# Reordering the tail of an attention-pooling kernel: a last load in two halves, and a different order of TensorE's closing steps

## The chip, the cores and the metric

The kernel runs on one core of one Trainium2 chip. The metric is the device time of one execution in microseconds (us), from the first to the last thing the core does; less is better.

## The reference

512 rows, each with 200 behaviours of 128 numbers and one candidate of 128 numbers. For each row an attention over the 200 behaviours is computed, the behaviours are summed with its weights, and the sum goes with the candidate through a small two-layer network to one logit.

```python
B, S, E = (512, 200, 128)             # ATT_H = 128, MLP_H = 256, all float32
W_b, W_c = (fc1_w[:E], fc1_w[E:])
h = relu(einsum('bse,eh->bsh', behavior_emb, W_b) + (candidate_emb @ W_c)[:, None, :] + fc1_b)
scores = einsum('bsh,h->bs', h, fc2_w[:, 0]) + fc2_b[0]
attn = softmax(scores, axis=-1)
user_interest = einsum('bse,bs->be', behavior_emb, attn)
x = concatenate([user_interest, candidate_emb], axis=1)
z = relu(x @ mlp1_w + mlp1_b)
logit = (z @ mlp2_w + mlp2_b)[:, 0]
```

## The kernel before

**Tiling.** The 512 rows are taken in 32 chunks of 16 rows (`CHUNKS` is 32, `LAST` is 31). Each chunk is loaded twice, 1.6 MB each time: once transposed (`xt`, for the first product and the scores) and once in its own layout (`x`, 128 partitions of 25 tiles of 128 numbers, for the weighted sum). SyncE issues both kinds from one queue, four buffers of each kind. The own layout of a chunk is loaded by `load`, which waits until the sum of the chunk four earlier has released its buffer.

**The loop.** In the period of chunk c TensorE does the first product of chunk c (`products`), the scores of chunk c-1 and the weighted sum of chunk c-3. ScalarE and VectorE make the high and low halves of the transposed data, the relu and the softmax. GpSimd spreads the exponentials over a block mask (`mask_weights`), so that a matmul with them as weights sums each row apart. Every second chunk the sums are copied from PSUM to SBUF by ScalarE (`copy_pooled4`), folded and transposed by a product with a mask (`transpose_sums`), and copied again (`copy_pooled_t`).

**The tail.** After the loop every engine has its own order written out by hand; it runs it strictly as written, and semaphores alone tie the engines together. The rows are in two parts (`PART_CHUNKS`): part 0 is chunks 0 to 27 (448 rows), part 1 is chunks 28 to 31 (64 rows). For each part TensorE does:

- `row_sums` (L702): sums of the exponentials; VectorE then takes reciprocals and spreads them (`inverses`, L502 and L505), and `spread_inverses` (L708) brings them to all partitions.
- `mlp_candidates` (L721): the candidate's half of the first layer, for m = 0 and 1 (two halves of the 256 hidden units).
- `normalise` on VectorE (L515): the transposed sums times the inverses.
- `mlp_pooled` (L727): the pooled half of the first layer, onto the same banks, then a relu: on ScalarE for part 0 (`relu`, L378), on VectorE for part 1 (`last_relu`, L572).
- `logits` (L734), then an add on VectorE (L589) and a store issued by SyncE (L279), for part 0 first.

`weighted_sum_alone` does the sums of chunks 30 and 31, which fill one bank between them; each is one call of `sum_tiles` over 25 tiles, or two calls for the last chunk (13 tiles, then the rest). Its weights come from `mask_last` on VectorE (L564), in the same two runs. Then the last chain starts: `copy_pooled4(LAST)`, `transpose_sums(LAST)`, `copy_pooled_t(LAST)`, `normalise(1)`, `mlp_pooled(1, m)`, `last_relu`, `logits(1)`, the add, the store. One float32 matmul stands in the trace as two records of MATMUL (PE) and two of LDWEIGHTS (PEld).

Of the kernel before, what the change touches and what calls it, by code (L numbers as in the profile page):

```python
# [7 lines left out]
ALU = mybir.AluOpType  # L8
# [3 lines left out]
P = 128  # L12
# [3 lines left out]
ROWS = P // PARTS  # L16
# [6 lines left out]
TILES = 25  # L23
# [12 lines left out]
LAG = 3  # L36
# [24 lines left out]
def attention_pooling_kernel(nc, behavior, behavior_t, cand_rest, weights_1, first, masks, later, out):  # L61
# [13 lines left out]
    with ExitStack() as ctx:  # L75
# [3 lines left out]
        def sem(name):  # L79
            return ctx.enter_context(nc.semaphore(name))  # L80
# [71 lines left out]
        xt_loaded = [sem(f"xt_loaded{i}") for i in range(XT_BUFS)]  # L152
        x_loaded = [sem(f"x_loaded{i}") for i in range(X_BUFS)]
        xt_half = sem("xt_half")
        weights_1_loaded = sem("weights_1_loaded")
        first_loaded = sem("first_loaded")
        masks_loaded = sem("masks_loaded")
# [73 lines left out]
        @block.sync  # L231
        def _(sp):
            arrivals = [*xt_piece, xt_loaded[0]]
            for g, arrived in enumerate(arrivals):
                sp.dma_start(xt[0][:, g, :], behavior_t[0, :, g, :]).then_inc(arrived, 16)
            sp.dma_start(cand_t[:, P:], cand_rest).then_inc(cand_rest_loaded, 16)
            for half, arrived in enumerate([xt_half, xt_loaded[1]]):
                mine = slice(2 * half, 2 * half + 2)
                sp.dma_start(xt[1][:, mine, :], behavior_t[1, :, mine, :]).then_inc(arrived, 16)
                if half == 0:  # L240
                    sp.dma_start(masks_sb[:, :], masks).then_inc(masks_loaded, 16)

            def load_transposed(c, buf):


                if buf is None:
                    buf = c
                elif isinstance(c, int) and c < XT_BUFS + WHOLE:
                    sp.wait_ge(z_done, (c - XT_BUFS + 1) * GROUPS)
                else:  # L250
                    sp.wait_ge(xl_made, (c - XT_BUFS + 1 - WHOLE) * GROUPS)
                sp.dma_start(xt[buf][:, :, :], behavior_t[c, :, :, :]).then_inc(xt_loaded[buf], 16)

            def load(c, buf):

                if buf is None:
                    buf = c
                else:
                    sp.wait_ge(pooled_done, c + (1 - X_BUFS))
                sp.dma_start(x[buf][:, :], behavior_v[c, :, :]).then_inc(x_loaded[buf], 16)  # L260


            for c in range(2, X_BUFS):
                load_transposed(c, None)
            load(0, None)
            sp.dma_start(later_sb[:, :], later).then_inc(later_loaded, 16)
            for c in range(X_BUFS, 2 * X_BUFS):
                load_transposed(c, c - X_BUFS)
                load(c - LAG, None if c - LAG < X_BUFS else c - LAG - X_BUFS)
            with sp.Fori(0, CHUNKS // X_BUFS - 2) as turn:  # L270
                for j in range(X_BUFS):
                    c = turn * X_BUFS + (2 * X_BUFS + j)
                    load_transposed(c, j)
                    load(c - LAG, (j - LAG) % X_BUFS)
            for c in range(CHUNKS - LAG, CHUNKS):
                load(c, c % X_BUFS)
            for part, (a, b) in enumerate(PART_CHUNKS):
                sp.wait_ge(logit_made, part + 1)
                sp.dma_start(out[a * ROWS:b * ROWS].rearrange("(g n) -> g n", g=GROUPS),  # L279
                             logit[0:P:Q, part, 0:quarter[part]]).then_inc(stored, 16)  # L280
            sp.wait_ge(stored, 2 * 16)
# [31 lines left out]
        def _(act):  # L313
# [26 lines left out]
            def copy_pooled4(c, bank):  # L340
                act.wait_ge(pooled_done, c + 1)
                nc.scalar.copy(pooled4[:, :], bank[:, 0:P]).then_inc(pooled4_copied, 2)
# [72 lines left out]
            copy_pooled4(LAST - 2, u_ps)  # L415
            copy_pooled_t(LAST - 2, u_ps[:, P:P + 2 * ROWS])
            exponents(LAST, LAST % 2, False)
            copy_pooled4(LAST, last_pair_ps)
            copy_pooled_t(LAST, last_pair_ps[:, P:P + 2 * ROWS])
            relu(0)  # L420
            relu(1)

        @block.vector
        def _(dve):
# [130 lines left out]
                next_low(2)  # L555

            periods(period)(dve)
            def mask_last(run):
                a, b = [0, LAST_RUN, TILES][run:run + 2]
                buf = LAST % 2  # L560
                if run == 0:
                    dve.wait_ge(weights_made, LAST + 1)
                    dve.wait_ge(pooled_done, LAST - 1)
                nc.vector.tensor_tensor(  # L564
                    weights_by_row[buf][:, a:b, pair_half[buf]],
                    weights[buf][:, a:b].unsqueeze(2).to_broadcast([P, b - a, ROWS]),
                    row_mask.unsqueeze(1).to_broadcast([P, b - a, ROWS]), ALU.mult).then_inc(last_masked, 1)

            def last_relu(m):
                a, b = PART_CHUNKS[1]  # L570
# [5 lines left out]
            inverses(0, 2)  # L576
            for n in range(SOFTMAX_STEPS):
                softmax(LAST, LAST % 2, n, False)
            mask_last(0)
            mask_last(1)  # L580
            inverses(1, 1)
            normalise(0)
            inverses(1, 2)
            normalise(1)
            last_relu(0)
            last_relu(1)
            for part in range(2):
                dve.wait_ge(logit_done, part + 1)
                nc.vector.tensor_scalar(logit[:, part, 0:quarter[part]], logit_ps[part][:, 0:quarter[part]], b_out, None,  # L589
                                        ALU.add).then_inc(logit_made, 1)  # L590

        @block.tensor
        def _(pe):
# [73 lines left out]

            def weighted_sum_alone(c):
                q = c % X_BUFS
                pe.wait_ge(x_loaded[q], loads(c, q))  # L670
                if q % 2 == 0:

                    pe.wait_ge(relu_made, LAST * HALF + 1)
                    pe.wait_ge(masked, c + 1)
                    sum_tiles(c, q, last_pair_ps, 0, WHOLE_TILES, GROUPS - 1).then_inc(pooled_done, 1)
                else:
                    pe.wait_ge(last_masked, 1)
                    sum_tiles(c, q, last_pair_ps, 0, LAST_RUN, None)
                    pe.wait_ge(last_masked, 2)
                    sum_tiles(c, q, last_pair_ps, LAST_RUN, WHOLE_TILES, LAST_RUN).then_inc(pooled_done, 1)  # L680

            def transpose_sums(c, summed):
# [94 lines left out]
            score(LAST, LAST % 2, False)  # L777
            transpose_sums(LAST - 2, u_ps[:, P:P + 2 * ROWS])
            spread_inverses(0)
            weighted_sum_alone(LAST - 1)  # L780
            mlp_candidates(1, 0)
            row_sums(1)
            weighted_sum_alone(LAST)
            spread_inverses(1)
            mlp_candidates(0, 0)
            mlp_candidates(0, 1)
            mlp_candidates(1, 1)
            transpose_sums(LAST, last_pair_ps[:, P:P + 2 * ROWS])
            mlp_pooled(0, 0)
            mlp_pooled(0, 1)  # L790
            mlp_pooled(1, 0)
            mlp_pooled(1, 1)
            logits(0)
            logits(1)


# [50 lines left out]
```

## Time and profile before

| what | value |
|---|---|
| time, median of 3 runs | 266.75 us (266.53 to 266.75) |
| time of the profiled execution | 266.47 us |
| its span, first to last instruction | 264.7 us |
| PE busy | 259.3 us, 98% of the span |
| DVE busy | 224.2 us, 85% |
| ACT busy | 200.6 us, 76% |
| queue of the large loads, share of 16 DMA engines' span | 94.7% |
| share of the last chain on PE | 60% |
| granted TensorE clock, mean | 1.000 |

The span is what the profiler records from the first to the last instruction; the time has 1.8 us more around it. PE is TensorE's matmuls, PEld its weight loads, DVE VectorE, ACT ScalarE, SPq SyncE's queue. The ends of matmuls are modelled, so that a busy PE shows starts better than ends.

### The profile page before, as it was taken

The page shows a single profiled execution, that of the slowest core. Times are in us where ns is not written, and L with a number is a line of the kernel's source. Part 1 is how long each engine was busy: PE and PEld are TensorE (multiplying, and loading weights), DVE is VectorE, ACT ScalarE, POOL GpSimd, SP SyncE. Part 2 cuts the span into 40 slices and gives each one's busy share as a digit, 9 for nine tenths or more (in the row PEclk, how much of TensorE's full clock was granted, in tenths as well). Part 3 has the DMA queues.
Part 4 walks back from the last instruction along what each step waited for, and adds up shares of the span by engine and source line. Part 5 has one row for each costly group of instructions (what it writes and reads, how often), then busy time and mean ns, then how long its engine had stood idle before and what let it go on. Part 6 is the DMA issues. An engine that isn't in the chain of part 4 may idle for free.

```text
span 264.7 us, 10384 instructions
## 1 busy us (share of the span) xinstructions
PE 259.3 (98%) x3942; PEld 212.4 (80%) x3942; DVE 224.2 (85%) x397; ACT 200.6 (76%) x481; POOL 29.4 (11%) x38
## 2 busy tenths in 40 slices
PE   8999999999999999999999999999999999999995
PEld 7557788888888868888888888888888888888973
DVE  0479998999898988989899998989989898999541
ACT  2569888798887697878789887878888787889312
POOL 2003001111110111110111111011111100111100
PEclk9999999999999999999999999999999999999999
DMA  7999999999999999999999999999999999999900
GB/s 247 430 433 422 422 426 420 424 424 420 426 422 423 426 420 429 429 426 426 424 429 429 426 426 426 428 428 422 428 429 428 426 426 426 429 428 426 391 32 0
DMA packets 10544, 105.87 MB, mean 400 GB/s; under 512 B 1184, under 2 KB 1696, under 8 KB 2592
## 3 DMA queue, kind: packets, MB, share of 16 engines
q1 hardware_dynamic: 10240, 105.44, 94.7%
q8 instruction: 12, 0.20, 0.3%
q10 hardware_dynamic: 288, 0.20, 0.2%
q14 instruction: 4, 0.03, 0.0%
HBM read 105.63 MB, written 0.00 MB: 399 GB/s over the span
## 4 chain that ended last, share of the span: by engine, by line
PE 60%; DMA 18%; DVE 14%; issue 4%; ACT 1%; DVEq 1%; POOL 0%; ACTq 0%; SPq 0%; POOLq 0%
DMA xt<-in_behavior_t 18%; PE s_ps L632 12%; PE u_ps L643 11%; PE z_ps L617 10%; PE z_ps L613 9%; DVE xl L454 9%; PE z_ps L614 8%; DVE hidden L464 5%; PE z_ps L608 4%; PE z_ps L750 2%; PE z_ps L643 1%; ACT xh L329 1%; PE z_ps L684 1%; PE z_ps L727 1%; PE z_ps L721 1%
## 5 line engine op out<-in xcount | busy, mean ns | idle before, releaser
L454 DVE TENSOR_TENSOR xl<-xt,xh 128x800 fp32r<-128x800 f32 x120 | 123.2, 1047 | 8.9 <-ACT xh L329 8.7
L329 ACT CAST xh<-xt 128x800 fp32r<-128x800 f32 x120 | 100.4, 862 | 34.2 <-DMA xt<-in_behavior_t 33.1
L371 ACT ACTIVATE hidden<-z_ps,bias 128x200 f32<-128x200 f32 x256 | 88.3, 428 | 7.4 <-PE z_ps L608 3.6
L613 PE MATMUL z_ps<-xh,w_hi 128*128 128x512 f32 x240 | 86.4, 360 | 0.5 <-DVE hidden L464 0.5
L614 PE MATMUL z_ps<-xh,w_lo 128*128 128x512 f32 x240 | 79.4, 345 | 0.0
L464 DVE TENSOR_TENSOR hidden<-z_ps,neg_bias 128x800 f32<-128x800 f32 x64 | 62.9, 982 | 3.3 <-PE z_ps L608 2.0
L617 PE MATMUL z_ps<-xl,w_hi 128*128 128x512 f32 x240 | 64.8, 351 | 0.9 <-DVE xl L454 0.2
L613 PEld LDWEIGHTS z_ps<-xh,w_hi 128*128 128x128 f32 x240 | 45.0, 188 | 16.3 <-issue 6.0
L299 POOL TENSOR_TENSOR weights_by_row<-weights,masks_sb 128x400 f32<-128x400 f32 x31 | 27.6, 890 | 218.3 <-ACT weights L336 177.3
L632 PE MATMUL s_ps<-hidden,f_col 128*3 128x160 f32 (+4 forms) x1280 | 50.1, 301 | 0.0
L614 PEld LDWEIGHTS z_ps<-xh,w_lo 128*128 128x128 f32 x240 | 45.1, 188 | 5.6
L643 PE MATMUL u_ps<-x,weights_by_row 128*32 128x128 f32 (+1 forms) x1680 | 46.7, 262 | 0.0
L643 PEld LDWEIGHTS u_ps<-x,weights_by_row 128*32 128x32 f32 x1680 | 42.3, 110 | 1.1
L632 PEld LDWEIGHTS s_ps<-hidden,f_col 128*3 128x3 f32 (+4 forms) x1280 | 32.3, 90 | 11.6 <-issue 4.2
L617 PEld LDWEIGHTS z_ps<-xl,w_hi 128*128 128x128 f32 x240 | 38.0, 188 | 4.1 <-DVE xl L454 4.0
L475 DVE STREAM_TRANSPOSE scores<-s_ps 128x160 f32<-128x160 f32 x32 | 10.9, 339 | 3.3 <-PE s_ps L632 3.1
L336 ACT ACTIVATE weights<-scores,exp_bias 128x25 f32<-128x25 f32 x32 | 10.9, 340 | 3.3 <-DVE exp_bias L493 3.3
L608 PE MATMUL z_ps<-xt,weights_sb 128*128 128x512 f32 (+1 forms) x32 | 11.9, 516 | 0.0
L608 PEld LDWEIGHTS z_ps<-xt,weights_sb 128*128 128x128 f32 x32 | 6.1, 199 | 5.1 <-issue 4.4
L493 DVE SCALAR_TENSOR_TENSOR exp_bias<-row_max,shift 128x1 f32<-128x1 f32 x32 | 7.0, 220 | 3.4
L483 DVE STREAM_TRANSPOSE part_max_t<-part_max 128x32 f32<-128x32 f32 x32 | 6.8, 213 | 1.1
L489 DVE STREAM_TRANSPOSE row_max<-row_max_t 128x32 f32<-128x32 f32 x32 | 6.8, 212 | 1.1
(65 smaller groups left out, 77.6 us busy)
## 6 DMA issues: line engine op xcount, KB each, us to landing
x<-in_behavior SPq DMA_DIRECT2D x32, 1600.0 KB, 26.6
xt<-in_behavior_t SPq DMA_DIRECT2D x30, 1600.0 KB, 23.7
xt<-in_behavior_t SPq DMA_DIRECT2D x4, 400.0 KB, 4.9
xt<-in_behavior_t SPq DMA_DIRECT2D x2, 800.0 KB, 7.7
later_sb<-in_later SPq DMA_DIRECT2D x1, 258.5 KB, 19.6
first_sb<-in_cand_rest SPq DMA_DIRECT2D x1, 192.0 KB, 5.7
first_sb<-in_first ACTq DMA_DIRECT2D x1, 128.0 KB, 4.8
masks_sb<-in_masks SPq DMA_DIRECT2D x1, 114.0 KB, 6.8
```

The costliest lines, as they stand in the source:

```text
L299: nc.gpsimd.tensor_tensor(weights_by_row[buf][:, :, pair_half[buf]], weights[buf][:, :].unsqueeze(2).to_broadcast([P, TILES, ROWS]), row_m ...
L329: nc.scalar.copy(xh[g][:, :], xt[q][:, g, :]).then_inc(xh_made, 1)
L336: nc.scalar.activation(weights[buf][:, :].rearrange("p (r t) -> p r t", t=RUN), score_runs(buf), ACT.Exp, bias=exp_bias[buf][:, :], accum_ ...
L371: op = nc.scalar.activation(hidden[q % 2][:, g, :, mine], z[:, :, mine], ACT.Relu, bias=bias[:, bass.ds(c * ROWS + g * EACH + b, 1)])
L454: nc.vector.tensor_tensor(xl[g][:, :], xt[q][:, g, :], xh[g][:, :].bitcast(F32), ALU.subtract).then_inc(xl_made, 1)
L464: nc.vector.tensor_tensor(hidden[q % 2][:, g, :, :].rearrange("p t (b s) -> p t b s", s=PARTS), z, nb.to_broadcast([P, TILES, EACH, PARTS] ...
L608: op = nc.tensor.matmul(z[:, a:b], w_b, xt[q][:, g, a:b], start=True, stop=True)
L613: nc.tensor.matmul(z[:, a:b], w_hi[:, :], xh[g][:, a:b], start=True, stop=False)
L614: nc.tensor.matmul(z[:, a:b], w_lo[:, :], xh[g][:, a:b], start=False, stop=False)
L617: op = nc.tensor.matmul(z[:, a:b], w_hi[:, :], xl[g][:, a:b], start=False, stop=True)
L632: op = nc.tensor.matmul(s_ps[g * Q:g * Q + rows, 0:RUN * Q].rearrange("p (t s) -> p t s", s=Q), f2_col[:, 0:rows], hidden[buf][:, g, r * R ...
L643: return nc.tensor.matmul(bank[g * Q:(g + 1) * Q, cols], weights_by_row[buf][:, t, :], x[q][:, t * E + cols.start:t * E + cols.stop], star ...
```

## The change

The own layout of chunk 31 is loaded by two transfers instead of one: tiles 0 to 12 with a semaphore of their own (`x_half`), then tiles 13 to 24. `mask_last` makes the weights in one instruction instead of two. The orders of the tail change on three engines:

- TensorE: all four `mlp_candidates` stand ahead of the sum of chunk 30; `mlp_pooled(0, ·)`, `row_sums(1)` and `spread_inverses(1)` stand between the sums of chunks 30 and 31; `logits(0)` stands directly behind the sum of chunk 31, ahead of `transpose_sums(LAST)`.
- ScalarE: the two `relu` of part 0 stand ahead of the two last copies.
- VectorE: `normalise(0)` stands ahead of the mask, `inverses(1, ·)` follow it, and the add of part 0's logits stands ahead of `normalise(1)`.

```diff
@@ sync
-            for c in range(CHUNKS - LAG, CHUNKS):
+            for c in range(CHUNKS - LAG, LAST):
                 load(c, c % X_BUFS)
+            sp.wait_ge(pooled_done, CHUNKS - X_BUFS)
+            cols = LAST_RUN * E
+            sp.dma_start(x[LAST % X_BUFS][:, 0:cols], behavior_v[LAST, :, 0:cols]).then_inc(x_half, 16)
+            sp.dma_start(x[LAST % X_BUFS][:, cols:], behavior_v[LAST, :, cols:]).then_inc(x_loaded[LAST % X_BUFS], 16)
@@ scalar
             exponents(LAST, LAST % 2, False)
+            relu(0)
+            relu(1)
             copy_pooled4(LAST, last_pair_ps)
             copy_pooled_t(LAST, last_pair_ps[:, P:P + 2 * ROWS])
-            relu(0)
-            relu(1)
@@ vector
-            mask_last(0)
-            mask_last(1)
+            normalise(0)
+            mask_last()
             inverses(1, 1)
-            normalise(0)
             inverses(1, 2)
+            add_out_bias(0)
             normalise(1)
             last_relu(0)
             last_relu(1)
-            for part in range(2):
-                dve.wait_ge(logit_done, part + 1)
-                nc.vector.tensor_scalar(logit[:, part, 0:quarter[part]], logit_ps[part][:, 0:quarter[part]], b_out, None,
-                                        ALU.add).then_inc(logit_made, 1)
+            add_out_bias(1)
@@ tensor, weighted_sum_alone
-                pe.wait_ge(x_loaded[q], loads(c, q))
                 if q % 2 == 0:
+                    pe.wait_ge(x_loaded[q], loads(c, q))
...
                 else:
+                    pe.wait_ge(x_half, 16)
                     pe.wait_ge(last_masked, 1)
                     sum_tiles(c, q, last_pair_ps, 0, LAST_RUN, None)
-                    pe.wait_ge(last_masked, 2)
+                    pe.wait_ge(x_loaded[q], loads(c, q))
                     sum_tiles(c, q, last_pair_ps, LAST_RUN, WHOLE_TILES, LAST_RUN).then_inc(pooled_done, 1)
@@ tensor, the order
             spread_inverses(0)
+            for part in range(2):
+                for m in range(2):
+                    mlp_candidates(part, m)
             weighted_sum_alone(LAST - 1)
-            mlp_candidates(1, 0)
-            row_sums(1)
-            weighted_sum_alone(LAST)
-            spread_inverses(1)
-            mlp_candidates(0, 0)
-            mlp_candidates(0, 1)
-            mlp_candidates(1, 1)
-            transpose_sums(LAST, last_pair_ps[:, P:P + 2 * ROWS])
             mlp_pooled(0, 0)
             mlp_pooled(0, 1)
+            row_sums(1)
+            spread_inverses(1)
+            weighted_sum_alone(LAST)
+            logits(0)
+            transpose_sums(LAST, last_pair_ps[:, P:P + 2 * ROWS])
             mlp_pooled(1, 0)
             mlp_pooled(1, 1)
-            logits(0)
             logits(1)
```

## Rows read from the trace of the kernel before

**Rows 1.** Chain that ended last, in order of time: start us, us, what.
```profile
255.13 1.53 PE z_ps L643 x52
```

**Rows 2.** The issue of chunk 31's own layout, by line: duration ns, start us, time to landing.
```profile
L260 SPq DMA_DIRECT2D x<-in_behavior x1: 328/328/328, 238.7 to 238.7; - x1
DMA to landing us min/median/max: 15.3/15.3/15.3
```

**Rows 3.** Timeline of the tail, TensorE: start us, us, engine, line, op, tiles, count.
```profile
253.01 1.58 PE L643 MATMUL z_ps<-x,weights_by_row 128*32 128x128 f32 x56
254.52 0.43 PE L721 MATMUL s_ps<-first_sb,later_sb 128*128 128x64 f32 x2
254.79 0.34 PE L702 MATMUL z_ps<-weight_sums,masks_sb 128*128 128x4 f32 x2
255.06 1.60 PE L643 MATMUL z_ps<-x,weights_by_row 128*32 128x128 f32 x56
256.59 0.43 PE L708 MATMUL z_ps<-inv_sel,ones 128*128 128x64 f32 x2
256.86 1.72 PE L721 MATMUL z_ps<-first_sb,later_sb 128*128 128x448 f32 x4
258.42 0.33 PE L721 MATMUL u_ps<-first_sb,later_sb 128*128 128x64 f32 x2
258.59 0.36 PE L684 MATMUL z_ps<-masks_sb,pooled 128*128 128x32 f32 x2
258.78 1.75 PE L727 MATMUL z_ps<-pooled_n,later_sb 128*128 128x448 f32 x4
260.37 0.33 PE L727 MATMUL s_ps<-pooled_n,later_sb 128*128 128x64 f32 x2
260.86 0.87 PE L734 MATMUL z_ps<-z_all,later_sb 128*1 128x112 f32 x32
261.26 0.35 PEld L734 LDWEIGHTS z_ps<-z_all,later_sb 128*1 128x1 f32 x24 [0.30 <-ACT z_all L378]
```

**Rows 4.** Timeline of the tail, VectorE and ScalarE, columns as in the group above.
```profile
247.76 0.99 DVE L464 TENSOR_TENSOR hidden<-z_ps,neg_bias 128x800 f32<-128x800 f32 x1 [0.89 <-PE z_ps L617]
...
252.33 0.18 ACT L346 COPY pooled_t<-u_ps 128x32 f32<-128x32 f32 x1 [1.48 <-PE u_ps L684]
...
254.01 0.64 DVE L564 TENSOR_TENSOR weights_by_row<-weights,masks_sb 128x208 f32<-128x208 f32 x2 [0.50 <-ACT weights L336]
...
255.16 0.18 DVE L502 RECIPROCAL inv_sums<-z_ps 128x4 f32<-128x4 f32 x1 [0.51 <-PE z_ps L702]
255.26 0.60 DVE L515 TENSOR_TENSOR pooled_n<-z_ps,pooled_t 128x448 f32<-128x448 f32 x1
255.78 0.22 DVE L505 TENSOR_TENSOR inv_sel<-inv_sums,masks_sb 128x64 f32<-128x64 f32 x1
...
256.76 0.27 ACT L342 COPY pooled<-z_ps 128x128 f32<-128x128 f32 x1 [2.78 <-PE z_ps L643]
...
259.04 0.18 ACT L346 COPY pooled_t<-z_ps 128x32 f32<-128x32 f32 x1 [2.01 <-PE z_ps L684]
...
259.33 0.22 DVE L515 TENSOR_TENSOR pooled_n<-z_ps,pooled_t 128x64 f32<-128x64 f32 x1 [3.33 <-ACT pooled_t L346]
...
259.82 1.39 ACT L378 ACTIVATE z_all<-z_ps,later_sb 128x448 f32<-128x448 f32 x2 [0.59 <-PE z_ps L727]
...
260.74 0.28 DVE L572 TENSOR_SCALAR z_all<-s_ps,later_sb 128x64 f32<-128x64 f32 x1 [1.19 <-PE s_ps L727]
...
260.96 0.28 DVE L572 TENSOR_SCALAR z_all<-u_ps,later_sb 128x64 f32<-128x64 f32 x1
...
261.70 0.48 DVE L589 TENSOR_SCALAR logit<-z_ps,later_sb 128x112 f32<-128x112 f32 x2 [0.45 <-PE z_ps L734]
```

**Rows 5.** The two final adds and the two stores, by line: ns min/median/max, first and last start.
```profile
L589 DVE TENSOR_SCALAR logit<-z_ps,later_sb x2: 226/280/334, 261.7 to 261.9; 128x112 f32<-128x112 f32 x1, 128x16 f32<-128x16 f32 x1
L279 SPq DMA_DIRECT2D out_logit<-logit x2: 507/580/654, 262.1 to 262.8; - x2
```

More of the change, by code:

```diff
@@ L154, in attention_pooling_kernel @@
         xt_half = sem("xt_half")
+        x_half = sem("x_half")
         weights_1_loaded = sem("weights_1_loaded")
@@ L557, in _, with mask_last @@
             periods(period)(dve)
-            def mask_last(run):
-                a, b = [0, LAST_RUN, TILES][run:run + 2]
+            def mask_last():
                 buf = LAST % 2
-                if run == 0:
-                    dve.wait_ge(weights_made, LAST + 1)
-                    dve.wait_ge(pooled_done, LAST - 1)
+                dve.wait_ge(weights_made, LAST + 1)
+                dve.wait_ge(pooled_done, LAST - 1)
                 nc.vector.tensor_tensor(
-                    weights_by_row[buf][:, a:b, pair_half[buf]],
-                    weights[buf][:, a:b].unsqueeze(2).to_broadcast([P, b - a, ROWS]),
-                    row_mask.unsqueeze(1).to_broadcast([P, b - a, ROWS]), ALU.mult).then_inc(last_masked, 1)
+                    weights_by_row[buf][:, :, pair_half[buf]],
+                    weights[buf][:, :].unsqueeze(2).to_broadcast([P, TILES, ROWS]),
+                    row_mask.unsqueeze(1).to_broadcast([P, TILES, ROWS]), ALU.mult).then_inc(last_masked, 1)
             def last_relu(m):
@@ L578, in _, with add_out_bias @@
                 softmax(LAST, LAST % 2, n, False)
-            mask_last(0)
-            mask_last(1)
+            normalise(0)
+            mask_last()
             inverses(1, 1)
-            normalise(0)
             inverses(1, 2)
+            def add_out_bias(part):
+                dve.wait_ge(logit_done, part + 1)
+                nc.vector.tensor_scalar(logit[:, part, 0:quarter[part]], logit_ps[part][:, 0:quarter[part]], b_out, None,
+                                        ALU.add).then_inc(logit_made, 1)
+            add_out_bias(0)
             normalise(1)
```

## The prediction

> **What bounds the kernel now.** I read the page first, for the shares of the span: PE is busy nearly throughout, and the queue of the large loads is almost as full, so which of the two holds the end has to be read from the end itself. The chain that ended last says it: the sum of chunk 31 is on it as work of PE that begins where the PE work before it stops, at 255.13, and not behind a transfer [rows 1]. The load of chunk 31 was issued at 238.7 and landed 15.3 us later, at 254.0 [rows 2], while its first matmul began at 255.06, 0.27 behind the start of the instruction before it, the row sums of part 1 [rows 3]. That distance is what any such instruction takes to get past. So chunk 31's data were 1.1 us early. The weights for it, the mask on VectorE, were whole at 254.65 [rows 4], 0.4 early. What sets the tail is TensorE's own order: from 253.01 to 261.3 there is only one hole on it, the 0.30 ahead of the second half of the logits, where it waited for ScalarE's relu [rows 3]. The serial chain of the last chunk (copy, transpose, copy, normalise) runs meanwhile on the other engines under PE's candidate and pooled products of part 0, and so costs nearly nothing. I therefore rebuild the tail in the new order, instruction by instruction, from 253.01 on. Nothing before that moves: the load's issue at 238.7 is the first edit in time, and it has no other load behind it.
>
> **The transfers.** One issue becomes two, some 0.33 us more on SyncE's queue [rows 2], with only the stores behind them. The same bytes, so the second half lands at about 254.0. Bounds: nothing gained below, and above, if the smaller rows were slow, one landing more late by the whole 15.3. The first half was wanted at 255.06 and will be wanted at 259.2 (below), so I price it at nothing; the cover is now 5 us deep. Doing without cover, each us of lateness beyond it would cost a us.
>
> **The mask.** 208 and 192 elements took 0.64 in two instructions [rows 4]; one of 400 is less than the 0.60 that 448 elements take [rows 4]. `normalise(0)` (0.60) goes ahead of it, so the mask is ready about 0.6 us later, near 255.2. Wanted at 259.2: nothing. `normalise(0)` itself is ready near 254.2, or at the latest by 255.9 as before, and wanted at 256.46: nothing.
>
> **TensorE up to the sum of chunk 31.** The candidates may start at once: the last relu of VectorE on the bank ended at 248.75, and the copy that frees the last bank at 252.51 [rows 4]. From 253.01:
> - candidates: the four passes of 448 columns took 258.42 - 256.86 = 1.56, the two small products 0.21 and 0.17 [rows 3]. To 254.95.
> - sum of chunk 30: 254.52 - 253.01 = 1.51 [rows 3]. To 256.46.
> - `mlp_pooled(0, ·)`: 260.37 - 258.78 = 1.59 [rows 3]. To 258.05. The relus (0.63 each, two in 1.39 with their gap [rows 4]) begin 1.04 after its start as before (258.78 to 259.82), run from 257.5 to 258.9 and are done long before the logits.
> - `row_sums(1)` at 258.05. Here the new order makes a stall: `spread_inverses(1)` now follows it directly and needs VectorE's reciprocal and spreading of its result. Before, the whole sum of chunk 31 (1.53) stood between the two and covered this. Row sums to reciprocal 255.16 - 254.79 = 0.37; reciprocal 0.18; spreading 0.22 [rows 3, 4]; two hand-overs of 0.03 to 0.05, as from ScalarE's relu, done at 261.21, to PE at 261.26 [rows 3, 4]. Sum 0.85, so `spread_inverses(1)` starts at 258.90. Of this 0.27 is what the row sums took anyway; the stall is 0.58. Behind it waits the sum of chunk 31, which needs nothing of it. Bounds: 0.4 if the modelled ends of PE flatter the 0.37, 0.8 if each hand-over costs 0.1 more. I take 0.58, all of whose parts but the hand-overs have rows of the same instructions.
> - its 0.27 (256.59 to 256.86 [rows 3]) and the sum of chunk 31 starts at 259.17, 4.11 later than before.
>
> A rule of the Trainium skill bears on the stall: "TensorE: Matmul & The Clock Gate", The mechanism, says that TensorE can pull weight loads ahead of matmuls in flight when they go to another part of the array. Held against a semaphore wait it would have the first weights of the sum ready under the stall and give back an estimated 0.1 to 0.2. The row speaks against it: at 261.26 the weight loads of the logits too began only with the wait's end, after 0.30 of nothing [rows 3]. The sum goes by the row.
>
> **From there to the end.** Durations and distances are those of the same instructions before.
> - last matmul of the sum ends 1.60 after its start: 260.77. ScalarE's copy starts 0.10 later (256.66 to 256.76) and takes 0.27: 261.14. `logits(0)` fills this hole: its half of the first group took 0.30, the whole second batch of 24 loads 0.35 [rows 3], so it is issued by about 261.1 and costs nothing; without it PE would only idle. Its relus and inputs are ready.
> - transpose at 261.19; copy starts 0.45 after it (258.59 to 259.04) and takes 0.18: 261.82 [rows 3, 4].
> - `normalise(1)` 0.11 later, takes 0.22: 262.15 [rows 4]. The add of part 0's logits (0.33 [rows 5]), new in front of it on VectorE, runs from 261.2 to 261.5, before its input is there: nothing. Its store (0.65 [rows 5]) is out of the way by 262.3.
> - `mlp_pooled(1, 0)` at 262.20; relu 0.37 later (260.37 to 260.74), the second 0.22 after that and 0.28 long: 263.07 [rows 3, 4].
> - `logits(1)`, second half, at 263.12, result after 0.30: add at 263.42, 0.23 long [rows 5]: 263.65.
> - one store: issued at 263.68, 0.51 as the second one took, or 0.65 as the first [rows 5]: 264.19. From the end of the last issue (262.8 + 0.5 = 263.3) to the span's end at 264.7 it was 1.4: 265.6.
>
> **The sum.** Before, the end of chunk 31's sum (256.66) to the end of the span was 8.0; after, it is 265.6 - 260.77 = 4.8. So 3.2 are taken out behind the sum and 4.1 put in front of it. Of the 4.1, 3.5 is PE work that before filled the waits of the last chain; that chain is now bare. Net +0.9 us: 0.58 by the stall, the rest by waits that lie open after the transpose (262.20 against 261.4, when PE is free, and 262.6 to 263.1 for the relus), less what one store less at the very end saves (before, the second store was issued 0.7 behind the first). On the profiled execution that is 266.47 + 0.9 = 267.4; the median of the runs stands 0.28 above that execution, so the forecast is 266.75 + 0.9 = **267.7 us**, slower by 0.35%.
>
> **The rivals.** A measurement of this kernel tells some 0.2%, 0.53 us, from no change.
> - *A, the forecast: the bare chain and the stall, +0.9.* Its own range is 267.3 to 268.1: the stall at 0.4 or 0.8, the store's issue at 0.65 (+0.14), and a few hundredths on each of seven hand-overs either way. Chance 0.72.
> - *B, no change that can be told.* The hand-overs between engines in the new tail sum to some 0.5 (0.10, 0.05, 0.09, 0.11 and so on); were all 0.03, 0.3 would go, and with the stall at 0.4 the loss is 0.4: 267.2. For it speaks that the ends of matmuls are modelled; against it, that the starts on VectorE and ScalarE, which I used, are not. Chance 0.17.
> - *C, faster: the load was late after all.* This is one mechanism: if chunk 31's data land L us after 254.0, the kernel before pays L - 1.1 and the kernel after nothing until L is 5. It breaks even at L = 2.0 and is faster by over 0.2% from L = 2.5; at L = 3 the new kernel stands 1.0 below the old. Against it: all timed runs lie within 0.3 of the profiled one, in which it was 1.1 early, so none can have had an L above 1.4. With the L of 2.5 to 3 that a gain needs, the time would be some 266.0 against the 266.75. Chance 0.06. Perfetto Trace Analysis of the Trainium skill, DMA Optimizations, says that splitting a transfer can let work start sooner if DMA engines are generally idle. By that rule alone this rival would be favoured; the queue that is full to 94.7% of the span does not meet its condition, and the sum did not wait.
> - *D, much slower: the halves are slow.* If the shorter rows made the second half land after 259.2 plus the 0.8 that the first 13 tiles take, over 5 us late, every further us counts: with 2 us more 269.7. The rows of 12.8 KB become rows of 6.7 and 6.1 KB, and no row shown here has a loss of that kind. Chance 0.05.
>
> **How the numbers follow.** A, B, C and D have 0.72, 0.17, 0.06 and 0.05. Slower is A less the part of it under +0.53 (0.04), with D: 0.73. Within 0.2% is B with that part, less a part of B that is a small gain (0.03): 0.18. Faster is C with it: 0.09. The range reaches from 267.0, which leaves out C and a part of B, to 268.2, above A's own range and below D.
>
> **What would show it.** In the changed kernel's trace: the sum of chunk 31 starts at about 259.2, waiting for no DMA; TensorE is idle for about 0.6 ahead of L708's second use, released by VectorE's spreading; after the sum's end the chain is copy, transpose, copy, normalise, pooled, relu, logits, add, store, with PE idle for 0.8 ahead of the last pooled products and some 0.4 ahead of the last logits; the last add ends near 263.65 and the span is 265.6. The landing of both halves is over 4 us ahead of their use. The forecast is wrong if the stall or the bare chain is much shorter than its rows, if the old kernel in truth waited for the load, or if the split slows the queue by more than 5 us.

## The result, and the profile after

The changed kernel takes 267.72 us (median of 6 runs, 267.34 to 268.22); the kernel before 266.63 us (266.20 to 266.75) beside it. The ratio is 1.0046, 95% interval 1.0033 to 1.0060: slower by 1.2 us, or by 1.1 as the medians stand. Measured once more on another occasion it gave 1.0051 (1.0038 to 1.0064). The forecast was 267.7 us, slower by 0.35%.

First the tail of the changed kernel as a timeline, TensorE's weight loads left out, with the columns of [rows 3]. Lines have moved by a few: L649 is the weighted sum (L643 before), L709 the row sums, L715 the spreading of the inverses, L728 and L734 the candidate and the pooled products, L741 the logits, L691 the transpose.

```profile
252.95 1.67 PE L728 MATMUL z_ps<-first_sb,later_sb 128*128 128x448 f32 x4
...
254.04 0.58 DVE L567 TENSOR_TENSOR weights_by_row<-weights,masks_sb 128x400 f32<-128x400 f32 x1
...
254.94 1.58 PE L649 MATMUL z_ps<-x,weights_by_row 128*32 128x128 f32 x56
...
256.45 1.77 PE L734 MATMUL z_ps<-pooled_n,later_sb 128*128 128x448 f32 x4
...
258.06 0.28 PE L709 MATMUL z_ps<-weight_sums,masks_sb 128*128 128x4 f32 x2
...
258.37 0.18 DVE L507 RECIPROCAL inv_sums<-z_ps 128x4 f32<-128x4 f32 x1 [3.75 <-PE z_ps L709]
258.59 0.23 DVE L510 TENSOR_TENSOR inv_sel<-inv_sums,masks_sb 128x64 f32<-128x64 f32 x1
...
258.87 0.43 PE L715 MATMUL z_ps<-inv_sel,ones 128*128 128x64 f32 x2 [0.54 <-DVE inv_sel L510]
...
259.24 1.60 PE L649 MATMUL z_ps<-x,weights_by_row 128*32 128x128 f32 x56
...
260.63 0.59 PE L741 MATMUL z_ps<-z_all,later_sb 128*1 128x112 f32 x16
260.94 0.27 ACT L347 COPY pooled<-z_ps 128x128 f32<-128x128 f32 x1 [2.05 <-PE z_ps L649]
...
261.35 0.38 PE L691 MATMUL z_ps<-masks_sb,pooled 128*128 128x32 f32 x2
...
261.82 0.18 ACT L351 COPY pooled_t<-z_ps 128x32 f32<-128x32 f32 x1 [0.62 <-PE z_ps L691]
262.11 0.23 DVE L520 TENSOR_TENSOR pooled_n<-z_ps,pooled_t 128x64 f32<-128x64 f32 x1 [0.51 <-ACT pooled_t L351]
...
262.39 0.43 PE L734 MATMUL s_ps<-pooled_n,later_sb 128*128 128x64 f32 x2 [0.66 <-DVE pooled_n L520]
...
262.87 0.28 DVE L575 TENSOR_SCALAR z_all<-s_ps,later_sb 128x64 f32<-128x64 f32 x1 [0.53 <-PE s_ps L734]
...
263.20 0.45 PE L741 MATMUL z_ps<-z_all,later_sb 128*1 128x16 f32 x16 [0.15 <-DVE z_all L575]
263.72 0.23 DVE L589 TENSOR_SCALAR logit<-z_ps,later_sb 128x16 f32<-128x16 f32 x1 [0.35 <-PE z_ps L741]
```

TensorE now waits three times: 0.54 for VectorE's inverses, with the ready sum of chunk 31 queued behind it; 0.66 ahead of the last pooled products; 0.15 ahead of the last logits. A fourth gap, of 0.13 ahead of the transpose, is put down to no engine by the profile. Before, its only hole was 0.30 long [rows 3]. The sum of chunk 31 starts 4.18 later than in [rows 3] (259.24 against 255.06), and from its start to the last add's it is 4.5 against 6.8 (261.9 [rows 5] less 255.06): 2.4 won behind it, 4.2 paid in front. Of the 1.8 by which the last add is late, the store's issue, which no longer stands in a queue, gives back 0.6.

The two halves of the load, by line (duration ns, start us, time to landing):

```profile
L280 SPq DMA_DIRECT2D x<-in_behavior x1: 327/327/327, 238.8 to 238.8; - x1
...
DMA to landing us min/median/max: 13.5/13.5/13.5
...
L281 SPq DMA_DIRECT2D x<-in_behavior x1: 433/433/433, 239.2 to 239.2; - x1
...
DMA to landing us min/median/max: 14.9/14.9/14.9
```

They landed at 252.3 and 254.1; the whole chunk had landed at 254.0 [rows 2]. Split or whole, the last byte comes at the same time within 0.1, and now lies 5 us ahead of its use. The two stores, by line:

```profile
L284 SPq DMA_DIRECT2D out_logit<-logit x2: 508/572/636, 261.6 to 264.0; - x2
```

The first store is out of the way by 262.3, and the second starts straight behind the last add, where before it began 0.7 behind the first [rows 5].

### The profile page after: what moved, and what is told of

It reads as the page before. It is cut to its first block, busy times and chain, and to the rows that moved or that the text cites. A ratio compares the mean times of both kernels' runs of the same rounds, so it can differ in the third digit from the quotient of the medians.

```text
span 265.9 us, 10384 instructions
## 1 busy us (share of the span) xinstructions
PE 259.5 (98%) x3942; PEld 212.2 (80%) x3942; DVE 224.6 (84%) x396; ACT 199.9 (75%) x481; POOL 29.4 (11%) x38
## 4 chain that ended last, share of the span: by engine, by line
PE 75%; DMA 11%; DVE 10%; issue 2%; DVEq 0%; ACT 0%; SPq 0%; ACTq 0%
PE s_ps L638 15%; PE u_ps L649 13%; PE z_ps L623 13%; PE z_ps L619 13%; PE z_ps L620 11%; DMA xt<-in_behavior_t 9%; DVE xl L459 5%; PE z_ps L614 4%; DVE hidden L469 3%; DMA weights_sb<-in_weights 2%; PE z_ps L649 1%; PE z_ps L691 1%; PE z_ps L734 1%; PE z_ps L728 1%; PE z_ps L715 0%
## 5 line engine op out<-in xcount | busy, mean ns | idle before, releaser
L649 PE MATMUL u_ps<-x,weights_by_row 128*32 128x128 f32 (+1 forms) x1680 | 46.7, 262 | 0.0
L649 PEld LDWEIGHTS u_ps<-x,weights_by_row 128*32 128x32 f32 x1680 | 42.3, 110 | 1.1
```

Of the source, the lines that this page charges most:

```text
L649: return nc.tensor.matmul(bank[g * Q:(g + 1) * Q, cols], weights_by_row[buf][:, t, :], x[q][:, t * E + cols.start:t * E + cols.stop], star ...
```

## The experiments

Theory 1 is the prediction's: the loss is the stall ahead of `spread_inverses(1)` and the last chain, bare of TensorE work. Theory 2: one of the other edits costs the time, above all the split load with its shorter rows. Ratios are to the kernel before on the same chip.

**The split alone.** The kernel before, with chunk 31's load in two halves:

```diff
-            for c in range(CHUNKS - LAG, CHUNKS):
+            for c in range(CHUNKS - LAG, LAST):
                 load(c, c % X_BUFS)
+            sp.wait_ge(pooled_done, CHUNKS - X_BUFS)
+            cols = LAST_RUN * E
+            sp.dma_start(x[LAST % X_BUFS][:, 0:cols], behavior_v[LAST, :, 0:cols]).then_inc(x_half, 16)
+            sp.dma_start(x[LAST % X_BUFS][:, cols:], behavior_v[LAST, :, cols:]).then_inc(x_loaded[LAST % X_BUFS], 16)
@@ weighted_sum_alone
-                pe.wait_ge(x_loaded[q], loads(c, q))
                 if q % 2 == 0:
+                    pe.wait_ge(x_loaded[q], loads(c, q))
...
                 else:
+                    pe.wait_ge(x_half, 16)
                     pe.wait_ge(last_masked, 1)
                     sum_tiles(c, q, last_pair_ps, 0, LAST_RUN, None)
                     pe.wait_ge(last_masked, 2)
+                    pe.wait_ge(x_loaded[q], loads(c, q))
```

> The kernel before with nothing changed but the load of chunk 31, which comes in two halves, with their two waits. Theory 1 (the loss is the bare chain and the stall on TensorE): the second half still lands near 254, over 1 us ahead of its use, so within 0.2 us of the kernel before. Theory 2 (the two shorter-rowed transfers cost the time): most of the 1.1 us is here, 267.4 to 267.9 us.

Measured 266.77 us, ratio 1.0013 (1.0004 to 1.0022). That is 0.3 us more, a small but distinguishable part, not the 1.1 of theory 2. Its trace does not show a place for it. The second half's landing, by line, and the sum's start in the timeline:

```profile
L281 SPq DMA_DIRECT2D x<-in_behavior x1: 434/434/434, 239.2 to 239.2; - x1
...
DMA to landing us min/median/max: 14.9/14.9/14.9
```

```profile
255.13 1.60 PE L648 MATMUL z_ps<-x,weights_by_row 128*32 128x128 f32 x56
```

Landing at 254.1, start at 255.13, no wait: the span was the 264.7 of before. Since the next run but one has the same split and stands at 1.0003, and their intervals overlap, I do not take the 0.3 as shown to be the split's.

**The stall.** The changed kernel, with the row sums one step earlier:

```diff
+            row_sums(1)
             mlp_pooled(0, 0)
             mlp_pooled(0, 1)
-            row_sums(1)
             spread_inverses(1)
```

> The changed kernel with row_sums(1) moved ahead of mlp_pooled(0, m), so that VectorE's reciprocal and spreading run under 1.6 us of TensorE's work. Theory 1: the idle time of 0.54 us ahead of spread_inverses(1) is gone and everything behind it comes 0.5 to 0.6 us earlier, 0.5 us faster than the changed kernel. Rival (TensorE's idle time there is not on the path, because a transfer or the weights hold the sum of chunk 31): under 0.2 us.

Measured 267.11 us, ratio 1.0024 (1.0015 to 1.0033), against 1.0046 and 1.0051 for the changed kernel: 0.6 to 0.7 us given back, about the size of the hole, and 0.1 more than expected. The timeline of TensorE there, spreading and then sum:

```profile
258.46 0.33 PE L715 MATMUL z_ps<-inv_sel,ones 128*128 128x64 f32 x2
...
258.72 1.60 PE L649 MATMUL z_ps<-x,weights_by_row 128*32 128x128 f32 x56
```

No wait stands behind L715, and the sum starts at 258.72 instead of 259.24. The rival, for which the sum had been held by something else, falls. Here the two weight loads of the spreading began apart, at 258.08 and 258.46; in the changed kernel both began only with the wait's end:

```profile
258.87 0.30 PEld L715 LDWEIGHTS z_ps<-inv_sel,ones 128*128 128x128 f32 x2 [0.62 <-DVE inv_sel L510]
```

**The bare chain.** The changed kernel, with all its other edits, but TensorE's work put back behind the sum of chunk 31. ScalarE's relus and VectorE's add of part 0's logits also go back to their old places, which this cut does not show:

```diff
             weighted_sum_alone(LAST - 1)
-            mlp_pooled(0, 0)
-            mlp_pooled(0, 1)
             row_sums(1)
-            spread_inverses(1)
             weighted_sum_alone(LAST)
-            logits(0)
+            spread_inverses(1)
+            mlp_pooled(0, 0)
             transpose_sums(LAST, last_pair_ps[:, P:P + 2 * ROWS])
+            mlp_pooled(0, 1)
             mlp_pooled(1, 0)
             mlp_pooled(1, 1)
+            logits(0)
             logits(1)
```

> The changed kernel with the split load, the one mask, the early normalise(0) and the early candidates kept, but mlp_pooled(0, m), spread_inverses(1) and logits(0) put back behind the sum of chunk 31, where they lie under the last chain, and the orders of ScalarE and of the two last adds put back with them. Theory 1: both the stall and the bare chain are gone, within 0.2 us of the kernel before, 1.1 us faster than the changed one. Theory 2 (transfer, mask or candidates cost the time): it stays at the changed kernel's 267.7.

Measured 266.60 us, ratio 1.0003 (0.9994 to 1.0012): the whole loss is gone, with the split load, the single mask, the early `normalise(0)` and the early candidates still in. This is the run that decides between the theories. With the run before it, it also divides the loss: 0.6 to 0.7 us for the stall (1.0046 or 1.0051 to 1.0024), and 0.6 for the bare chain (1.0024 to 1.0003). In its timeline the last chain again runs under work:

```profile
258.57 0.27 ACT L347 COPY pooled<-z_ps 128x128 f32<-128x128 f32 x1 [4.46 <-PE z_ps L649]
...
258.67 0.97 PE L734 MATMUL z_ps<-pooled_n,later_sb 128*128 128x448 f32 x2
...
259.48 0.30 PE L691 MATMUL z_ps<-masks_sb,pooled 128*128 128x32 f32 x2
...
259.62 1.00 PE L734 MATMUL z_ps<-pooled_n,later_sb 128*128 128x448 f32 x2
259.87 0.19 ACT L351 COPY pooled_t<-z_ps 128x32 f32<-128x32 f32 x1 [1.04 <-PE z_ps L691]
...
260.45 0.42 PE L734 MATMUL s_ps<-pooled_n,later_sb 128*128 128x64 f32 x2
```

The copy lies under the spreading and the first pooled product, the second copy and `normalise(1)` under the second. From the sum's start (256.87 in that trace) to the last add's it is 5.1, longer than the 4.5 of the changed kernel, and yet the whole is faster, as the sum starts 2.4 earlier: a shorter chain behind the sum is not the aim, a TensorE without holes is.

**Where logits(0) stands.** The run on the stall, with `logits(0)` behind the transpose:

```diff
             weighted_sum_alone(LAST)
-            logits(0)
             transpose_sums(LAST, last_pair_ps[:, P:P + 2 * ROWS])
+            logits(0)
```

> The changed kernel with row_sums(1) early, as in the run on the stall (267.1), and logits(0) moved from ahead of transpose_sums(LAST) to behind it, where TensorE otherwise waits 0.8 us for VectorE. If logits(0) held up the transpose, which began 0.14 us behind the end of ScalarE's copy where 0.05 would do, this gives back 0.1 us: 267.0. If the transpose waits for the copy alone, no difference from 267.1.

Measured 267.52 us, ratio 1.0028 (1.0018 to 1.0038): no gain. The expected 0.1 was wrong on its premise, since the hand-over from the copy to the transpose stayed 0.14 with nothing in front of it. Against the run on the stall it is 0.1 to 0.2 slower (1.0028 and 1.0024), which the intervals do not tell apart. Something new came in the profiled execution, at 267.70 one of the slower ones, seen in the timelines of the three engines:

```profile
260.51 0.27 ACT L347 COPY pooled<-z_ps 128x128 f32<-128x128 f32 x1 [1.13 <-PE z_ps L649]
...
260.92 0.38 PE L691 MATMUL z_ps<-masks_sb,pooled 128*128 128x32 f32 x2 [0.51 <-ACT pooled L347]
...
261.39 0.18 ACT L351 COPY pooled_t<-z_ps 128x32 f32<-128x32 f32 x1 [0.62 <-PE z_ps L691]
261.86 0.33 DVE L589 TENSOR_SCALAR logit<-z_ps,later_sb 128x112 f32<-128x112 f32 x1 [4.29 <-PE z_ps L741]
262.11 0.21 DVE L520 TENSOR_TENSOR pooled_n<-z_ps,pooled_t 128x64 f32<-128x64 f32 x1
```

The copied sums were there at 261.57, but `normalise(1)` is queued behind the add of part 0's logits, which waits for TensorE: 0.4 lost in this trace. The add put behind `normalise(1)` again:

```diff
-            add_out_bias(0)
             normalise(1)
+            add_out_bias(0)
```

> As the run with logits(0) behind transpose_sums(LAST), but VectorE's add of part 0's logits stands behind normalise(1) again. There the add ran from 261.86 to 262.11 and normalise(1), whose input was there near 261.6, began only behind it. If that was what ate the gain, this is 0.3 to 0.4 us faster than that kernel: a ratio of about 1.0015 to before, and no more than 0.1 better than with row_sums(1) early alone. If the copy's hand-over to the transpose sets it, no difference.

Measured 267.01 us, ratio 1.0016 (1.0008 to 1.0025), 0.3 us below the run before it as expected, though the two intervals overlap, so that the times alone do not show it. Against the run on the stall (1.0024) it is 0.2 better, with overlap again. In its trace `normalise(1)` starts at 261.57, 0.10 behind the copy. Against the kernel before, what is left is, by the reading above, the bare chain.

**How deep the cover of the load is.** One more load of 1.6 MB, into a buffer that nobody reads, ahead of chunk 31's in the queue; once in the kernel before (the edit below) and once in the changed one, ahead of its two halves:

```diff
+        scratch = sb("scratch", [P, TILES * E])
...
@@ sync
-            for c in range(CHUNKS - LAG, CHUNKS):
+            for c in range(CHUNKS - LAG, LAST):
                 load(c, c % X_BUFS)
+            sp.dma_start(scratch[:, :], behavior_v[0, :, :]).then_inc(dummy_loaded, 16)
+            load(LAST, LAST % X_BUFS)
...
+            sp.wait_ge(dummy_loaded, 16)
             sp.wait_ge(stored, 2 * 16)
```

> The kernel before with one more load of 1.6 MB into a buffer that nobody reads, queued directly ahead of chunk 31's own layout. At some 425 GB/s it takes 3.8 us, so chunk 31 lands near 257.8 instead of 254.0. If the cover of this load was 1.1 us, as read from the trace of before, the kernel is 2.7 us slower, 269.1 to 269.4. If the load had already been the limit, 3.8 us slower, 270.3.

Measured 271.18 us (269.80 to 272.35), ratio 1.0191 (1.0172 to 1.0209). The median lies above both values expected, and the spread is 2.5 us where it is at most 1.0 elsewhere. The profiled execution, at 269.80, is the fastest and the only one near what was expected; its rows by line and in the timeline:

```profile
DMA to landing us min/median/max: 19.3/19.3/19.3
```

```profile
258.32 1.61 PE L648 MATMUL z_ps<-x,weights_by_row 128*32 128x128 f32 x56 [3.01 <-DMA x<-in_behavior]
```

The load, issued at 238.9, landed at 258.2, 4.2 late, and TensorE waited 3.0 for it: the cover was 1.1 to 1.2, as read from [rows 2, 3]. The span was 3.3 longer. The other four runs took 1.3 to 2.6 us more still, with mean granted TensorE clocks of 0.987 to 0.994 where the profiled one has 0.998. As an estimate from these means and the spans, they miss 3.0, 1.6, 3.0 and 1.1 us of full clock more than the profiled one does, and they took 2.3, 1.4, 2.6 and 1.3 us longer. So a clock that fell while TensorE still had work, to 1.2 instead of 2.4 GHz, is the likely cause of the excess; when it fell was not seen. The one trace has it fall only behind the last matmul, as its stretches show (us; busy time of each engine; PEclk, DMA share, GB/s):

```profile
262.00:265.00 3.00, 2.96 (x43) 1.76 (x41) 0.77 (x4) 1.45 (x3) 0.00 (x0) 1.00 0.00 0
265.00:268.00 3.00, 0.00 (x0) 0.00 (x0) 0.44 (x2) 0.00 (x0) 0.00 (x0) 0.81 0.00 1
```

> The changed kernel with the same additional load of 1.6 MB ahead of chunk 31's two halves, which then land near 257.8, while the sum of chunk 31 starts at 259.2. Theory 1 (the cover is now 5 us deep and its price is the bare chain): no slower than the changed kernel, 267.7. Rival D (the halves are on the path): up to 3.8 us slower, 271.

Measured 267.58 us, ratio 1.0039 (1.0026 to 1.0052): not slower than the changed kernel at all. The second half, issued at 239.0, needed 18.8 and landed at 257.8, still 1.3 ahead of the sum's start:

```profile
259.07 1.61 PE L653 MATMUL z_ps<-x,weights_by_row 128*32 128x128 f32 x56
```

So the change does buy something: 4 us more of cover for the last load. On this kernel nothing needs it, and it costs 1.1 us. Where the load is 4 us late the changed kernel wins by 3.6 by the medians (271.18 and 267.58), and by 2.2 against the one execution of the old kernel whose clock did not fall.

**The end of the end.** The kernel before, its second store issued from ScalarE's queue:

```diff
+        def store(eng, part):
+            a, b = PART_CHUNKS[part]
+            eng.wait_ge(logit_made, part + 1)
+            eng.dma_start(out[a * ROWS:b * ROWS].rearrange("(g n) -> g n", g=GROUPS),
+                          logit[0:P:Q, part, 0:quarter[part]]).then_inc(stored, 16)
@@ sync
-            for part, (a, b) in enumerate(PART_CHUNKS):
-                sp.wait_ge(logit_made, part + 1)
-                sp.dma_start(out[a * ROWS:b * ROWS].rearrange("(g n) -> g n", g=GROUPS),
-                             logit[0:P:Q, part, 0:quarter[part]]).then_inc(stored, 16)
+            store(sp, 0)
             sp.wait_ge(stored, 2 * 16)
@@ scalar, last
+            store(act, 1)
```

> The kernel before with the store of the last 64 rows issued from ScalarE's queue instead of SyncE's. From the rows of before, the second issue began at 262.8 because the first one, 0.65 us long, stood in front of it, while its data were there at 262.2. If the end is set by the issue and what follows it, the span is 0.5 us shorter, 266.1. Rival (the two stores share what they wait for, or ScalarE issues more slowly): within 0.2 us.

Measured 266.42 us, ratio 1.0000 (0.9991 to 1.0009). No gain; the two issues in the timeline:

```profile
262.21 0.64 SPq L234 DMA_DIRECT2D out_logit<-logit  x1
262.36 1.29 ACTq L234 DMA_DIRECT2D out_logit<-logit  x1
```

The issue from ScalarE took 1.29 and ended at 263.65, 0.35 later than two issues in a row on SyncE (263.3 [rows 5]), and yet the span was no longer (264.6 against 264.7): from the end of the last issue to the end of the span it was 0.95 here and 1.4 in the kernel before. So the recorded end of an issue is not by itself what sets the end. Then one store instead of two, with the logits of all rows in one bank, so that one add serves both:

```diff
@@ tensor, logits
-                    for g in range(GROUPS):
-                        op = nc.tensor.matmul(logit_ps[part][g * Q:g * Q + 1, 0:quarter[part]], w_out[:, m:m + 1],
-                                              z_all[:, m, bass.ds(PART_CHUNKS[part][0] * ROWS + g * quarter[part],
-                                                                  quarter[part])],
+                    first, last = (n * ROWS for n in PART_CHUNKS[part])
+                    for g in range(first // P, GROUPS):
+                        a, b = max(first, g * P), min(last, (g + 1) * P)
+                        op = nc.tensor.matmul(logit_ps[0][g * Q:g * Q + 1, a - g * P:b - g * P], w_out[:, m:m + 1],
+                                              z_all[:, m, a:b],
@@ vector (the two adds go)
...
+            dve.wait_ge(logit_done, 2)
+            nc.vector.tensor_scalar(logit[:, 0, :], logit_ps[0][:, 0:P], b_out, None, ALU.add).then_inc(logit_made, 1)
@@ sync (the two stores go)
...
+            sp.wait_ge(logit_made, 1)
+            sp.dma_start(out.rearrange("(g n) -> g n", g=GROUPS), logit[0:P:Q, 0, :]).then_inc(stored, 16)
+            sp.wait_ge(stored, 16)
```

> The kernel before with all 512 logits in one bank (part 1's 16-column pieces become one piece of 64 in the same bank), one add and one store instead of two of each. Two store issues of 0.65 and 0.51 us stood one behind the other, and issuing the second from ScalarE's queue did not help, as it took 1.3 us beside the first. Theory: the store's issue starts as before, about 262.1, and nothing is queued behind it: the span ends 0.5 us earlier, 265.9 to 266.0. Rival (a store of 128 columns is issued or lands more slowly, or the 0.5 is lost in what follows): within 0.2 us.

Measured 266.07 us, ratio 0.9979 (0.9971 to 0.9988): 0.6 us faster than before. The store was issued at 262.46 and not at 262.1 as expected, since it now waits for the one add, and the issue ended at 263.11. From the start of the logits to the end of the span the trace has 3.4 us (264.5 - 261.12) against 3.8 before (264.7 - 260.86 [rows 3]), which places 0.5 of the 0.6. The same on top of the order of the run on the bare chain:

> The changed kernel with mlp_pooled(0, m) and spread_inverses(1) back behind the sum of chunk 31 (266.6, as before) and with the one add and one store of the run that gave 0.6 us. If the two are independent, the gain is the same 0.5 to 0.6 and perhaps 0.1 more, since TensorE's last hole was 0.21 there and not 0.30: 266.0. If the gain came from another order of the old kernel's end, it is not here: 266.6.

Measured 265.90 us, ratio 0.9976 (0.9967 to 0.9986), the fastest of all, though not distinguishable from the run above. The end of its timeline:

```profile
261.92 0.35 DVE L589 TENSOR_SCALAR logit<-z_ps,later_sb 128x128 f32<-128x128 f32 x1 [0.47 <-PE z_ps L736]
262.30 0.64 SPq L283 DMA_DIRECT2D out_logit<-logit  x1
```

The one issue ends at 262.94, against 263.3 for the second of two [rows 5], and the span is 264.4 against 264.7: this trace, of an execution at 266.15, places 0.3 of the gain.

The changed kernel was also run once more, beside the kernel above and the one with the add behind `normalise(1)`:

> The changed kernel once more, on the same chip as the two below: its ratio to the kernel before was 1.0046 (1.0033 to 1.0060); by theory 1 it stands some 1.0 to 1.2 us above before, and 0.5 to 0.6 above the kernel with row_sums(1) early.

Measured 267.93 us, ratio 1.0051 (1.0038 to 1.0064), 1.3 us above before, just over the 1.0 to 1.2 expected, and 0.9 above the kernel with the row sums early, `logits(0)` and the add moved, measured beside it; 0.5 to 0.6 was expected to the run on the stall, which was not in this measurement.

## Why the prediction was right

The direction, the two causes and the size came out as forecast: +0.9 us, measured +1.1 to 1.2. That the forecast of 267.7 meets the measured 267.72 is partly luck. It was reckoned on a median of 266.75 for the kernel before, and the kernel before measured beside the changed one had 266.63; the lower base and the 0.2 to 0.3 by which the loss was under-priced hide each other in part.

**The bound.** The sum of chunk 31 was read as waiting for TensorE's order and not for the load, with 1.1 us to spare. The late-load run measured that cover: 4.2 late, 3.0 waited. Rivals C (the load was late after all) and D (the halves are slow) are out: the split alone lands at 254.1, and no kernel without the extra load waited for a transfer there. (For D the prediction has "over 5 us late"; by its own numbers, 259.2 + 0.8 - 254.0, it is 6.) Rival B (hand-overs so short that the loss drowns) is out too: they were longer than taken, not shorter.

**TensorE up to the sum.** Forecast start 259.17, measured 259.24. Candidates to 254.94 (254.95 forecast), sum of chunk 30 to 256.45 (256.46), row sums at 258.06 (258.05), spreading at 258.87 (258.90). These times flatter it a little, as the tail of this trace began 0.06 earlier than in the kernel before (252.95 against 253.01). The stall was priced at 0.58, TensorE's rows have 0.54, and removing it gave 0.6 to 0.7. The weight loads of the sum were not pulled under the wait: with the wait over at 258.87, TensorE took 0.37 until the sum began, 0.10 more than the 0.27 taken from the rows, and the loads of the spreading's own weights, which nothing had to compute, began only at 258.87 too. By the rule of the Trainium skill that the prediction weighed ("TensorE: Matmul & The Clock Gate", The mechanism) 0.1 to 0.2 of that might have gone; this trace agrees with the rows of before and does not show weight loads pulled ahead past a wait for another engine.

**From the sum to the end.** Forecast 4.8 from the end of the sum to the end of the span, measured 265.9 - 260.84 = 5.1. Two hand-overs to TensorE were under-sized: copy to transpose 0.14 instead of 0.05, and start of the pooled products to the relu 0.48 instead of 0.37. With 0.07 at the sum's start these make up most of the 0.30 by which the last add is late (263.72 against 263.42). For the second the rows of the weight loads show where the 0.11 lies, first before, then in the changed kernel:

```profile
260.00 0.19 PEld L727 LDWEIGHTS s_ps<-pooled_n,later_sb 128*128 128x128 f32 x1 [0.19 <-issue]
...
262.39 0.30 PEld L734 LDWEIGHTS s_ps<-pooled_n,later_sb 128*128 128x128 f32 x2 [0.77 <-DVE pooled_n L520]
```

Before, the first of the two loads began 0.37 ahead of its matmul, under the one before; in the changed kernel both begin with the matmul. It is this and not a hole on TensorE that goes with the longer distance: in the run on the bare chain TensorE has no hole ahead of that matmul, but its loads waited for VectorE too and both began with it (260.44), and the relu came 0.47 behind it. The row sums agree: 0.31 to the reciprocal in the changed kernel, whose first load began 0.38 ahead, 0.42 in the run on the stall, whose loads began with the matmul. For the first, the 0.05 was itself the distance behind a wait (of 0.30, for the relu), so the wait is not the difference; the run with `logits(0)` behind the transpose shows the 0.14 again with nothing in front. There the weights are the very sums that ScalarE has just copied. What makes the 0.09 stays open. So the term "a few hundredths on each of seven hand-overs" was the one mis-sized: 0.3 us in all, and the loss of the profiled execution is 1.2 instead of 0.9. TensorE's holes on this chain came out shorter than forecast, 0.66 and 0.15 against 0.8 and 0.4; their lengths hang on the modelled ends of the matmuls, the sum above goes by starts.

**The edits at nothing.** The mask was ready at 254.62 (254.04 + 0.58), half a us sooner than feared, as `normalise(0)` ran under the wait for the exponentials. It was never wanted before 259.2. The split, mask, early `normalise(0)` and early candidates together cost nothing that is measurable (1.0003). The add of part 0's logits in front of `normalise(1)` is free only while `logits(0)` comes early: in the trace of the run with it behind the transpose it cost 0.4.

**The stores.** One issue less at the end was reckoned as a saving of some 0.7 in the changed kernel; in the trace it gave back 0.6. The run with one store gets 0.6 in the old order, without the new one.

Left open: the 0.3 us of the split alone, which no row places; the 0.09 between copy and transpose; why the store's issue on ScalarE's queue took 1.29; and where the clock fell in the four slower runs with the late load.

## What to carry to other kernels

Moving work from behind the last data to the front of them pays only if those data are late; here they were 1.1 us early, and the work moved had been the filling of the last chain (copy, transpose, copy, normalise). Look for the instruction whose answer comes back to the same engine (here row sums, reciprocal, spreading) and keep other work between the two, and do not put a waiting instruction in front of one that is ready: that cost 0.6 here. At the very end count the stores: two in a row cost 0.6 us more here than one of the whole.

## What the runs showed of the hardware

- A store issued on ScalarE's queue 0.15 us behind one on SyncE's took 1.29 us to issue, against 0.51 for a second one on SyncE's own queue [rows 5]. From the end of the first issue (262.85) to its own it was 0.80. That the two queues cannot issue side by side does not follow: at the start of the same trace ScalarE's queue issued two loads in 0.41 and 0.46 us (from 0.76 on) while SyncE's issued four (0.75 to 2.57). Why this one was long was not tested. The Trainium skill says in "Trainium Kernel Development and Optimization", Key Constraints, that issuing from several engines saves the sequencers' issue time; this run shows no such saving for two small stores.
- Splitting a load of 12.8 KB rows into rows of 6.7 and 6.1 KB in a full queue left the landing of the last byte where it was (254.1 against 254.0).
- TensorE started 0.05 us behind ScalarE's end when its next weights were a single column [rows 3, 4], and 0.14 behind when the weights were the 128 columns that had just been copied (weight load 0.11 behind). Behind VectorE's end it was 0.05 with 128 columns of weights that had lain ready (262.34 to 262.39), so the number of columns alone does not make it.
- Where the first of a matmul's two weight loads began about 0.4 us ahead of it, the next engine started 0.31 (row sums) and 0.37 (pooled products) behind its start; where both loads began with it, 0.42 and 0.48. No weight load began ahead in the changed kernel while TensorE waited for another engine.
- In the kernel whose one trace has a wait of 3 us, four of five executions had a mean granted clock of 0.987 to 0.994, and were 1.3 to 2.6 us slower than the fifth; with holes of up to 0.7 us the clock's level in the timed runs stayed at 0.995 and above.
